# A graph-and-experts kernel: the end of the third list's sort moved from the second ranking into the small aggregation, and tile sizes loaded as 16-bit values

## What is computed

```python
edge_index = jnp.stack([src, dst])
x = x + _L0_gnn_ref(_layernorm(x, axis=-1), edge_index, L0_gnn_W, L0_gnn_a_left, L0_gnn_a_right)
x = x + _L0_ffn_ref(_layernorm(x, axis=-1)[None], L0_ffn_W_gat, ..., L0_ffn_edge_index)[0]
x = x + _L1_gnn_ref(_layernorm(x, axis=-1), edge_index, L1_gnn_weight, L1_gnn_att_src, L1_gnn_att_dst, L1_gnn_bias)
x = x + _L1_ffn_ref(_layernorm(x, axis=-1)[None], L1_ffn_router_w, L1_ffn_w1, L1_ffn_w2, L1_ffn_w3)[0]
```

## Time and profile before

| | us |
|---|---|
| median of 3 runs | 9118.15 (9117.16 to 9119.92) |
| span of the profiled execution | 10110.4 |
| large aggregation, in the profile | 1003 to 3679 |
| second ranking | 3679 to 4246 |
| small aggregation | 4246 to 5812 |
| last aggregation | 6312 to 8850 |

### The profile page before, as it was taken

The page is one execution under the profiler, slowest core; times in us unless marked ns, Lnnn a source line. Parts: engine busy times, 40 slices in busy tenths (PEclk is TensorE's granted clock), DMA queues, the critical chain, the costliest instruction groups (busy, mean ns, idle before and its releaser), DMA issues. The chain is left out here.

```text
span 10110.4 us, 54577 instructions
## 1 busy us (share of the span) xinstructions
PE 2288.8 (23%) x9111; PEld 1752.0 (17%) x9112; DVE 5594.3 (55%) x8828; ACT 1093.7 (11%) x2533; POOL 5337.1 (53%) x5411
## 2 busy tenths in 40 slices
PE   2112000000000002146555512000000000129995
PEld 1111000000000001135444411000000000116663
DVE  8764588788777677523333275455656556421111
ACT  1101000000000001112222201000000000002221
POOL 0025656666676654455555345776666777542221
PEclk7555555555555555578777755555555555559997
DMA  4051333433333353411111162433333333620004
GB/s 142 22 159 50 97 82 87 122 99 98 101 101 98 102 113 74 122 23 33 29 28 28 30 172 89 109 100 92 101 98 101 106 99 99 129 97 30 30 30 117
DMA packets 458121, 869.43 MB, mean 86 GB/s; under 512 B 175134, under 2 KB 294860, under 8 KB 448192
## 3 DMA queue, kind: packets, MB, share of 16 engines
q0 software_dynamic: 239536, 575.99, 23.0%
q1 hardware_dynamic: 167648, 182.04, 6.2%
q10 hardware_dynamic: 50788, 110.02, 3.3%
HBM read 693.35 MB, written 180.71 MB: 86 GB/s over the span
## 5 line engine op out<-in xcount | busy, mean ns | idle before, releaser
L914 POOL DMA_INDIRECT agg_ring<-table,agg_idx x4320 | 4275.8, 990 | 2329.8 <-issue 1323.4
L1042 DVE TENSOR_TENSOR agg_part<-agg_ring,agg_prob 128x2048 f32 x420 | 964.4, 2296 | 631.8 <-issue 556.2
L1080 DVE TENSOR_TENSOR agg_wide<-agg_wide,agg_part 128x2048 f32<-128x2048 f32 x420 | 960.4, 2287 | 14.4
L1786 PE MATMUL dense_tp<-all_ident,dense_xn 128*128 128x128 f32 x100 | 23.9, 425 | 2570.3 <-issue 2543.7
L1408 PE MATMUL agg_hp<-agg_xt,agg_w 128*128 128x256 f32 x1600 | 446.4, 439 | 579.4 <-ACT agg_ht L1378 340.3
L2208 DVE TENSOR_TENSOR experts_h<-experts_sg,experts_hp 128x682 f32<-128x682 f32 x106 | 91.8, 866 | 779.7 <-ACT experts_sg L2191 779.7
L2158 PE MATMUL experts_hp<-mixture_w,experts_xt 128*128 x1696 | 518.2, 458 | 0.6 <-ACT experts_xt L2187 0.6
L1408 PEld LDWEIGHTS agg_hp<-agg_xt,agg_w 128*128 128x128 f32 x1600 | 352.4, 224 | 663.8 <-ACT agg_ht L1378 360.4
L1786 PEld LDWEIGHTS dense_tp<-all_ident,dense_xn 128*128 128x128 f32 x100 | 20.3, 228 | 2571.9 <-issue 2544.5
L2129 POOL DMA_INDIRECT yc<-experts_ysb,experts_list x105 | 103.7, 987 | 685.2 <-DVE experts_ysb L2217 685.2
L1422 PE MATMUL agg_yp<-agg_w,agg_ht 128*128 128x256 f32 x1600 | 405.3, 411 | 231.0 <-remote 174.5
(11 more groups left out here) (421 smaller groups left out, 6520.8 us busy)
## 6 DMA issues: line engine op xcount, KB each, us to landing
agg_ring<-table,agg_idx POOLq DMA_INDIRECT x4320
y<-agg_ysb ACTq DMA_DIRECT2D x25, 1024.0 KB
rank_y<-y SPq DMA_DIRECT2D x10, 2560.0 KB
rank_x<-x SPq DMA_DIRECT2D x30, 640.0 KB
copies<-first_sort_words SPq DMA_DIRECT2D x16, 1024.0 KB
copies<-last_sort_words ACTq DMA_DIRECT2D x16, 1024.0 KB
x<-rank_x SPq DMA_DIRECT2D x20, 640.0 KB
agg<-agg_res ACTq DMA_DIRECT2D x98, 128.0 KB
```

The costliest lines, as they stand in the source:

```text
L914: pool.indirect_dma_start(out=self.ring[:, to:to + self.RW], out_offset=None, in_=self.table, in_offset=bass.IndirectOffsetOnAxis(ap=index ...
L1042: return dve.tensor_tensor(to[:, :].rearrange("p (j h c) -> p j h c", j=UNIT, h=H), ring[:, ds(st.at(at_u), UNIT * RW)].rearrange("p (j w) ...
L1080: dve.tensor_tensor(wide[:, :], wide[:, :], part[:, :], ALU.add).then_inc(widened, 1)
```

## The change

Two things. First, the second ranking loses the third list's sort (no `after`), and so its PSUM tile, its steps and its store. Steps 112 to 192 are given to `aggregate_small` as a `Beside` with one share (`SHARES = 1`) and a window of 512 columns. DVE runs all of them behind tile 0; PE runs the turns ahead of its first block; ACT runs the copies of the turns and the store behind tile 0 and ahead of the first half block; ACT waits for the store to land at the stage's end. The buffers of `sorts[2]` stay allocated for that long. Second, `aggregate` keeps six 16-bit values per tile instead of five 32-bit ones: `c0` is split into its high part and its low 4 bits by two more DVE operations, and the engines put it together again in registers.

```diff
@@ class Beside
-    def __init__(self, parts=()):
+    def __init__(self, parts=(), window=1024):
@@
-            turned = s.ps("words_turned", [P, 1024])
+            turned = s.ps("words_turned", [P, self.window])
@@
 EARLY = 112
+SHARES = 1
+LOAD = 6
@@ aggregate
-        sizes = s.sb("sizes", [1, 5 * (NT + 1)], I32)
+        sizes = s.sb("sizes", [1, LOAD * (NT + 1)], mybir.dt.uint16)
+        bits, split = s.sb("bits", [1, 2 * (NT + 1)], I32), s.sem("split")
@@
-            ng, nk, c0, k0, missing = nc.values_load_multi_w_load_instructions(sizes[0:1, ds(t * 5, 5)], engines=[eng.engine], min_val=0, max_val=cfg.max_slots,
-                                                                      skip_runtime_bounds_check_because=why)[1]
-            return nc.s_assert_within(ng, 1, CH, skip_runtime_bounds_check_because=why), nk, c0, k0, missing
+            ng, nk, c_high, c_low, k0, missing = nc.values_load_multi_w_load_instructions(
+                sizes[0:1, ds(t * LOAD, LOAD)], engines=[eng.engine], min_val=0, max_val=cfg.max_slots, skip_runtime_bounds_check_because=why)[1]
+            return nc.s_assert_within(ng, 1, CH, skip_runtime_bounds_check_because=why), nk, c_high * SLOTS + c_low, k0, missing
@@
+                dve.tensor_scalar(bits2[:, :, 0], st.inf[:, I_C0:I_C0 + NT + 1], 4, None, ALU.logical_shift_right).then_inc(split, 1)
+                dve.tensor_scalar(bits2[:, :, 1], st.inf[:, I_C0:I_C0 + NT + 1], SLOTS - 1, None, ALU.bitwise_and).then_inc(split, 1)
...
+                dve.wait_ge(split, 2)
+                dve.tensor_copy(of_tile[:, :, 2:4], bits2[:, :, :]).then_inc(sized, 1)
@@ aggregate_small
+        share.allocate(s)
@@ on DVE
-                tile(0, None)
-                with dve.Fori(0, NT // 2) as i:
+                def pair(i):
                     tile(i * 2 + 1, None)
                     tile(i * 2 + 2, lambda: ffn.vector(dve, i))
+
+                tile(0, None)
+                share.vector(dve, 0)
+                for i in range(SHARES - 1):
+                    pair(i)
+                    share.vector(dve, i + 1)
+                with dve.Fori(SHARES - 1, NT // 2) as i:
+                    pair(i)
@@ on PE
-                with pe.Fori(0, NTP // 2) as b:
+                for b in range(SHARES):
+                    share.tensor(pe, b)
+                    ffn.tensor(pe, b)
+                with pe.Fori(SHARES, NTP // 2) as b:
                     ffn.tensor(pe, b)
@@ on ACT
+                tile(0)
+                share.scalar(nc, act, 0)
+                ffn.scalar(act, 0, 0)
+                store(0)
...
+                share.end_scalar(act)
@@ build
-            rank(1, after=sorts[2], done=EARLY, beside=dense[1])
...
+            rank(1, beside=dense[1])
...
+            rest = Beside([(sorts[2], EARLY, len(sorts[2].so.steps), 0, SHARES)], 512)
+            aggregate_small(nc, lists[1][0], 4, 4, tabs[1], infos[1], ells[1], outs[1], S, ffn, rest)
```

More of the change, by code:

```diff
@@ L918 @@
 class Beside:
-    def __init__(self, parts=()):
+    def __init__(self, parts=(), window=1024):
         self.parts = parts
+        self.window = window
         self.cuts = []
@@ L929, in allocate @@
         if self.parts:
-            turned = s.ps("words_turned", [P, 1024])
+            turned = s.ps("words_turned", [P, self.window])
             for ls, lo, hi, first, last in self.parts:
-                ls.so.turned, ls.so.window = turned, 1024
+                ls.so.turned, ls.so.window = turned, self.window
     def begin_vector(self, dve):
@@ L1166, in _, with aggregate_small @@
                 beside.end_scalar(act)
-def aggregate_small(nc, cfg, H, C, table, info, ell, out, S, ffn):
+def aggregate_small(nc, cfg, H, C, table, info, ell, out, S, ffn, share):
     CW = H * C
@@ L1315, in store, with pair @@
                     act.dma_start(out[ds(t * P, P), :] if not isinstance(t, int) else out[t * P:(t + 1) * P, :], res[:, :]).then_inc(out_stored, 16)
-                tile(0)
-                ffn.scalar(act, 0, 0)
-                store(0)
-                with act.Fori(0, NT // 2) as i:
+                def pair(i):
                     tile(i * 2 + 1)
@@ L1324, in _, with rest @@
                     tile(i * 2 + 2)
+                def rest(i):
                     ffn.scalar(act, i + 1, 0)
                     store(i * 2 + 2)
+                tile(0)
+                share.scalar(nc, act, 0)
+                ffn.scalar(act, 0, 0)
+                store(0)
+                for i in range(SHARES - 1):
+                    pair(i)
+                    share.scalar(nc, act, i + 1)
+                    rest(i)
+                with act.Fori(SHARES - 1, NT // 2) as i:
+                    pair(i)
+                    rest(i)
                 ffn.scalar(act, NT // 2, 1)
                 ffn.store(act, NT // 2)
+                share.end_scalar(act)
                 act.wait_ge(out_stored, NT * 16)
@@ L1379, in scalar @@
                 last.then_inc(self.gelu, 1)
-        if half == 1 and not isinstance(b, int):
+        if half == 1 and not (isinstance(b, int) and b == NT // 2):
             act.wait_ge(self.xt_used, b + 1)
@@ L2326, in build @@
                 aggregate(nc, lists[0][0], 8, 32, tabs[0], infos[0], ells[0], outs[0], True, S, share)
[L2327 to L2329 removed]
+            rank(1, beside=dense[1])
+            ffn = SmallExperts(xt1, a["L0_ffn_W1"], a["L0_ffn_b1"], a["L0_ffn_W2"], a["L0_ffn_b2"], y1, S)
+            rest = Beside([(sorts[2], EARLY, len(sorts[2].so.steps), 0, SHARES)], 512)
+            aggregate_small(nc, lists[1][0], 4, 4, tabs[1], infos[1], ells[1], outs[1], S, ffn, rest)
         rank(2, beside=dense[2])
```

11 lines of the change are left out of this document (5 added, 6 removed).

## The result

The changed kernel takes 9190.17 us (median of 4 runs, 9189.65 to 9195.17) against 9117.65 us for the kernel before on the same chip: ratio 1.0081, 95% interval 1.0069 to 1.0094, or 72.5 us slower. The forecast was 9239 us, 121 us slower, with a range of 9140 to 9320. Sign and range held. The size was missed by 49 us, and three steps of the argument were wrong.

What follows compares the result with a forecast made beforehand. The prediction took DVE to bound the second ranking and a DVE, ACT and PE chain the small aggregation. Second ranking -142, behind tile 0 +270, sizes -7 gave +121 on 9118, so 9239 us, range 9140 to 9320.

Steps and rivals of the forecast that it cites:

- second ranking: Without the third list's sort it was to lose 142 us: search 46, groups 63, end 33.
- behind tile 0: In the small aggregation, 235 us of sort steps and 35 us of store issue were to add 270 us.
- sizes: Loading a tile's sizes as six 16-bit values in the large aggregation was to save 7 us.
- The piece: Steps 112 to 192 behind tile 0: 176 us of DVE operations and 59 us of turns, 235 us.
- The store's issue: ACT issuing sixteen copies and two smaller transfers behind tile 0, ahead of tile 1's exponentials: 35 us.
- Delay passes whole: Small aggregation: a chain of 44 us a pair paces it against POOL's 31, so all 270 us reach the total.
- Rival 1: POOL paces the small aggregation and the ring takes 76 us of the delay: +194, 9163 us in all; chance 0.14.
- 992 us are the recording's own: The profiled span of 10110.4 us exceeds the 9118.15 us median only through recording, which stretches the late stages.
- The worst case I named: Sizes loads cost one price per register, six at 292 ns, 1.75 us against 1.05: plus 34 us.

Runs made afterwards that it cites:

- e2: The changed kernel with the turns' PSUM window at 2048 columns instead of 512, on the slow chip: 10218.91 us, ratio 1.0081 to the kernel before.
- e1: The kernel before with only the six 16-bit sizes per tile, the sort left in the second ranking, on the slow chip: 10137.68 us, ratio 1.0008.
- e9: The changed kernel with the turns' PSUM window at 2048 columns instead of 512, on a quick chip: 9170.89 us, ratio 1.0057 to the kernel before.
- e10: The changed kernel with ACT issuing the store behind pair 16, the piece still behind tile 0: 9160.3 us, ratio 1.0043 to the kernel before.
- e5: The kernel before with only the six 16-bit sizes per tile, on a quick chip: 9146.1 us, ratio 1.0025.
- e8: The changed kernel with twelve shares behind pairs 8 to 19 and five 16-bit sizes instead of six: 8990.7 us, ratio 0.9858 to the kernel before.
- e6: The changed kernel with ten shares behind pairs 12 to 21 instead of one piece, on a quick chip: 9055.63 us, ratio 0.9924 to the kernel before.
- e4: The changed kernel with ten shares behind pairs 12 to 21 instead of one piece, on the slow chip: 10225.91 us, ratio 1.0093 to the kernel before.

## Why the prediction was right or wrong, point by point

| term | forecast | measured (quick chips) |
|---|---|---|
| second ranking | -142 (-168 to -116) | -159 |
| behind tile 0 | +270 (246 to 281) | +208 |
| sizes | -7 (-22 to 0) | +23 |
| sum | +121 | +72 = -159 + 208 + 23; the result is +72.5 |

**The second ranking.** Right in mechanism: search 81 us as forecast, the groups held by POOL. Of the 17 us, 9 lie in the groups (201 to 129, 72 in place of 63) and 10 in the end (119 to 76, 43 in place of 33). For the groups the chip is the likely cause: I took their 148 us from the first ranking of the earlier trace rows, and in the profile after that same, unchanged stretch takes 126 us:

```profile
764.00:890.00 126.00, 51.10 (x193) 41.63 (x192) 80.88 (x264) 30.02 (x88) 95.74 (x99) 0.67 0.24 69
```

On the slow chip the groups came to 148 us and the end to 84, as forecast (148 and 86). But the stretch between search and groups grew there from 67 to 87 us, so e2's ranking was 447 us and e1's 573, 126 less and not 142.

**The piece.** Right: 234.5 us against 235, turns 7.24 against 7.3, and e9 confirms the window's price. The store's issue was put at 35 us; DVE waited 28.9 us for it, and e10's 35 with 20 either way can't choose between the two.

**"Delay passes whole".** Wrong on the chips of the result, and this is the step that failed. It rested on 44 us a pair against POOL's 31, and from that on "with the ring full then, before and after the change". The true pair of a quick chip is 35 us, and without the piece POOL never stands and the ring isn't full (365 gathers at tile 24 against 408 with it). So the ring took 264 - 208 = 56 us (234.5 + 28.9 of delay to tile 1's exponential, 208 passed), which is the 54 us of lead found above. Rival 1 had put 76 us to the ring and 9163 us in all: it counted the room left at tile 0. At tile 2 the changed kernel's POOL was indeed 56 gathers (70 us) ahead of e5's, but it stood twice more behind the piece with a full ring (49 and 8 us), while e5's went on, and from tile 8 on the lead was 43. With the right loads, 23 in place of -7, and the right ranking, it gives 9118 - 159 + 194 + 23 = 9176. I gave it 0.14. So the range held for a mechanism that I had held unlikely. On the slow chip the step holds from tile 2 on: the ring is full with and without the piece, and 203 to 215 us passed, in the late place as in front.

**"992 us are the recording's own".** Wrong. It was a guess that the two figures on the table (span and median) invited, and the rows could not test it. The 17 runs of the kernel before on the slow chip show that it really takes that long there. The Trainium skill, "NOTIFIC — the notification-queue block", section "7.1 Overflow: three behaviours, one of which stalls the engine", says only that a full queue of records can, in one of three settings, stall the engine that writes to it. That this stretched the late stages was my own step from it; no run here shows it. That the profiled run is no longer than the others of its group (9190.05 us against 9189.65 to 9195.17 after the change, 10145 against 10132 to 10161 in e1) speaks against it in this case. I drew half of the right conclusion, not to trust stage lengths after 4300 us, and then took the 44 us pair from that same stretch because its matmuls looked undisturbed. They were less disturbed, not undisturbed.

**The loads.** Wrong in sign. The worst case I named, one price per register, was the true mechanism, with 0.232 us a register where nothing adds to it (e8), not the 0.292 of a single load. 6 x 0.232 = 1.39 us against 1.05 before would make 17 us. In the large aggregation, where the loads count, they took more than that: 1.61 us in the mean of 49 in the profile after against 1.08 in the profile before (there is none of it from a quick chip), 49 x 0.53 = 26 us, and 23 are measured. The Trainium skill, "Runtime: NRT & Kernel Launch", section "Instruction fetch mechanics", says about 200 ns per register even in bulk; it speaks of registers loaded from device memory, and these values lie in the on-chip buffer. I set it aside because five 32-bit values take 591 or 1197 ns; for the 16-bit values the trace comes near it (232 ns). The row I had was of the other form.

The errors of +62 (behind tile 0) and -30 (loads) had opposite signs, and the ranking's error, +17, was on the side of the first, so 17 + 62 - 30 = 49 remained. That the sum came as near as it did is partly luck.

## What to carry to other kernels

A long piece of work put at one point of a stage costs what the stage's pacing engine stands for, so it belongs where that engine is slow and behind a buffer, in shares no larger than the buffer's slack: the same 81 steps cost 208 us in one piece behind tile 0 and 19 us in twelve shares behind pairs 8 to 19. Before pricing from a profile, ask whether the profile's execution is the one that is timed: here a span 11% over the median looks like another chip's, with another engine pacing the stage. And price a load into registers by its own form and in its own stage.

## What the runs showed of the hardware that was not expected

The same program took 9118 us on some chips and 10133 us on another, each steady within 0.5%. The time lies in a few stages. Between the profiles of e1 and e5, the same kernel, 1002 us differ: 200 in the large aggregation, 456 in the small one, 245 behind the third ranking, and nothing in the first sort (571 and 573 us). In the last aggregation a register instruction of DVE took 698 ns against 211 on a quick chip. The profile after shows the latter:

```profile
L1053 DVEq FUSED_REGOPS  x544: 46/211/304, 5700.0 to 7742.7; - x182
```

The cause is open. The ratio of the change to before was 1.0081 and 1.0085 on two quick chips, but a variant that was 0.8% faster there (e6) was 0.9% slower on the slow one (e4). For a choice between placements, the chip counted for more than the placement.

On quick chips loads of 16-bit values into registers took 232 ns each in the last aggregation, without regard to where they begin (1382 to 1401 ns for nearly all loads of six). In the large aggregation of the profile before, five 32-bit values took about 591 ns in every fourth tile and about 1190 in the others, as the prediction read it. Neither holds everywhere: in the last aggregation the median of DVE's loads was 702 ns for five 32-bit values (profile before) and 701 for six 16-bit ones (e1, slow chip):

```profile
L1006 DVEq TENSOR_LOAD <-agg_sizes x47: 604/702/1387, 6423.3 to 8661.4; - x47
...
L1011 DVEq TENSOR_LOAD <-agg_sizes x48: 4/701/1397, 6417.0 to 8686.5; - x48
```
